# The output projection and first norm of a latent attention, moved into the block of its pairs

## The reference

```python
x = x + _layernorm(_L0_attn_ref(_layernorm(x), Wq_a, q_a_ln_w, Wq_b, Wkv_a, kv_a_ln_w, Wkv_b, Wo))
x = x + _layernorm(_L0_ffn_ref(_layernorm(x), ...))
...
# _L0_attn_ref: 32 heads, no mask but causal (1024 x 1024)
q = _rmsnorm(h @ Wq_a, q_a_ln_w) @ Wq_b                  # split in q_nope (128) and q_pe (64, rotary)
compressed, k_pe = split(h @ Wkv_a)                      # 64 + 64
kv = _rmsnorm(compressed, kv_a_ln_w) @ Wkv_b             # split in k_nope and v
probs = softmax(where(causal, q . k * scale, min))
return (probs @ v).reshape(s, 32 * 128) @ Wo
```

## Time and profile before

| | us |
|---|---|
| median of 3 runs (lowest, highest) | 1609.5 (1608.85, 1614.17) |
| profiled execution: span from its first to its last instruction | 1606.4 |
| difference of that median and that span | 3.1 |
| TensorE busy in the span | 1492.6 (93%) |
| VectorE, ScalarE, GpSimd busy | 1023.0, 821.6, 291.7 |

### The profile page before, as it was taken

The page is one execution under the profiler, slowest core; times in us unless marked ns, Lnnn a source line. Parts: engine busy times, 40 slices in busy tenths (PEclk is TensorE's granted clock), DMA queues, the critical chain, the costliest instruction groups (busy, mean ns, idle before and its releaser), DMA issues. The chain is left out here.

```text
span 1606.4 us, 22430 instructions
## 1 busy us (share of the span) xinstructions
PE 1492.6 (93%) x8030; PEld 981.8 (61%) x8030; DVE 1023.0 (64%) x2013; ACT 821.6 (51%) x1487; POOL 291.7 (18%) x276
## 2 busy tenths in 40 slices
PE   6866999999999999977979999899899999999998
PEld 4645777766677776656868888787453333333355
DVE  5744666666666666643553343364687998999646
ACT  5325666666666666632221212223316777777854
POOL 2762111111211111100000000001410243342221
PEclk9987999999999999998989999999998999999999
DMA  4142222121212221124312111105730444430001
GB/s 138 53 193 73 76 75 69 64 69 64 69 63 80 90 70 40 34 86 156 105 63 75 59 60 40 53 1 152 189 67 5 68 81 79 80 67 15 19 11 53
DMA packets 63154, 116.57 MB, mean 73 GB/s; under 512 B 12814, under 2 KB 32398, under 8 KB 61758
## 3 DMA queue, kind: packets, MB, share of 16 engines
q1 hardware_dynamic: 62692, 114.23, 24.4%
q10 hardware_dynamic: 288, 0.79, 0.3%
q0 software_dynamic: 64, 0.11, 0.0%
HBM read 82.78 MB, written 29.66 MB: 70 GB/s over the span
## 5 line engine op out<-in xcount | busy, mean ns | idle before, releaser
L1882 DVE TENSOR_REDUCE ah_minus_half<-ah_ring 128x1 f32<-128x512 f32 x512 | 321.8, 680 | 58.5 <-PE ah_ring L1788 57.1
L968 DVE CUSTOM_DVE_ANT_0 mh_score<-mh_score,mh_mask 128x128 f32<-128x128 f32 (+7 forms) x256 | 195.9, 765 | 179.1 <-PE mh_score L781 179.0
L1852 ACT ACTIVATE ah_probs<-ah_score 128x1024 f32<-128x1024 f32 x256 | 248.7, 1024 | 69.5 <-PE ah_score L1805 68.8
L890 ACT ACTIVATE mh_probs<-mh_score,mh_minus_max 128x128 f32<-128x128 f32 (+7 forms) x256 | 189.8, 741 | 39.7 <-DVE mh_minus_max L968 35.7
L1788 PE MATMUL ah_ring<-ah_k_stack,ah_q_stack 48*128 48x512 f32 x512 | 179.1, 464 | 13.9 <-DMA ah_k_stack<-qk_scratch 5.5
L1788 PEld LDWEIGHTS ah_ring<-ah_k_stack,ah_q_stack 48*128 48x128 f32 x512 | 79.0, 187 | 173.1 <-DVE ah_minus_half L1882 158.9
L1041 POOL TENSOR_TENSOR h_lo<-mh_pe,h_hi 64x512 fp32r<-64x512 f32 x64 | 81.8, 1278 | 459.0 <-ACT h_hi L876 455.4
L1805 PE MATMUL ah_score<-ah_q_stack,ah_k_stack 49*128 49x512 f32 x512 | 156.5, 444 | 4.6 <-DMA ah_q_stack<-ah_rows 2.9
L779 PE MATMUL mh_score<-shared,h_hi 128*128 128x512 f32 (+3 forms) x384 | 152.0, 396 | 3.0 <-ACT mh_probs L890 2.9
L1820 PE MATMUL ah_mix<-ah_probs,ah_v 128*32 128x512 f32 x1024 | 139.0, 615 | 0.6 <-ACT ah_probs L1852 0.6
L781 PE MATMUL mh_score<-shared,h_lo 128*128 128x512 f32 (+3 forms) x384 | 133.0, 346 | 0.0
(11 more groups left out here) (227 smaller groups left out, 2898.7 us busy)
## 6 DMA issues: line engine op xcount, KB each, us to landing
mh_w<-in_w_pairs SPq DMA_DIRECT2D x16, 896.0 KB, 5.6
x<-in_w_inner SPq DMA_DIRECT2D x14, 768.0 KB, 4.2
pe_scratch<-fr_pe_out SPq DMA_DIRECT2D x4, 2048.0 KB, 6.6
mh_pe<-pe_scratch SPq DMA_DIRECT2D x16, 512.0 KB, 4.0
mh_spread<-inverse_scratch SPq DMA_DIRECT2D x64, 128.0 KB, 2.9
a_scratch<-mh_mixed SPq DMA_DIRECT2D x32, 256.0 KB, 2.4
x<-a_scratch SPq DMA_DIRECT2D x8, 1024.0 KB, 6.3
qk_scratch<-ai_ring SPq DMA_DIRECT2D x32, 256.0 KB, 2.8
```

What stands on the lines that cost most here:

```text
L890: nc.scalar.activation(probs[:, s % 2, 0:width], score_ps[s % 2][:, base:base + width], ACT.Exp, bias=minus_max[:, s % 4:s % 4 + 1], scale ...
L968: nc.vector.tensor_tensor_reduce(out=scores, in0=scores, in1=mask[:, S - width:S], scale=-1.0, scalar=3e38, op0=ALU.add, op1=ALU.min, accu ...
L1852: nc.scalar.activation(probs[:, 2 * (u % 2) + c, :], score_ps[c][:].rearrange("p e n -> p (e n)"), ACT.Exp, scale=MHA_SCALE).then_inc(prob ...
L1882: nc.vector.reduce_max(minus_half[:, m:m + 1], ring[:, m % 3, :], AX.X, negate=True).then_inc(max_taken, 1)
```

## The change

`mla_output` no longer opens a block. It returns a function `finish`, which `mla_heads` calls before its own block is opened; what `finish` returns is issued at the end of each engine's list, in the same block. Semaphores of the heads are not cleared in between, and there is no meeting of the engines. The tiles of the output stage lie at fixed places over buffers of the heads that are dead by then: `a_hi` and `a_lo` of tile 0 over `w`, `absorbed_hi`, `absorbed_lo`, `pe32` and the probabilities of even slots; those of tile 1, and `x`, over `high_turned`. The two score tensors' first banks take the products, the two turn tensors the transposes. Each first use waits for the last reader of the old content (`high_free`, `low_probs_free`, `mixed_free`, `all_stored`). VectorE makes tile 0's `a_lo` before it takes the last pair's second half. `x` is loaded in two parts, tile 0 and the rest.

In the last pair alone three places move: the transposed inverse of the first half from slot 10 to 9, `mix_low` from slot 14 to 10, and VectorE's `take_mix` of that half from slot 15 to 13.

```diff
-            return (i + 1, 2) if half else (i, 11 if i == 0 else 10)
+            return (i + 1, 2) if half else (i, 11 if i == 0 else 9 if i == LAST else 10)
+        def low_at(i):
+            return 10 if i == LAST else 14
+        def take_low_at(i):
+            return 13 if i == LAST else SLOTS - 1
...
+        def low_probs_free(engine):
+            engine.wait_ge(turns_ready, groups_before(LAST, SLOTS - 1))
+        def high_free(engine):
+            engine.wait_ge(mix_ready, 2 * PAIRS)
+        def mixed_free(engine):
+            engine.wait_ge(mix_taken, 2 * PAIRS)
+        def all_stored(engine):
+            engine.wait_ge(mixed_out, 16 * 2 * PAIRS)
+        banks = ([ps[:, 0:BANK] for ps in score_ps], turn_ps)
+        finish_sync, finish_gpsimd, finish_tensor, finish_scalar, finish_vector, prepare_vector = finish(
+            ctx, first, banks, low_probs_free, high_free, mixed_free, all_stored)
+        block = ctx.enter_context(nc.Block())
...
             store(LAST, 1)
-            sp.wait_ge(mixed_out, 16 * 2 * PAIRS)
+            finish_sync(sp)
...
-                    if s == 14:
+                    if s == low_at(i):
                         mix_low(i)
...
             mix_high(LAST, 0, NT)
+            finish_tensor(pe)
...
-                    if s == SLOTS - 1:
+                    if s == take_low_at(i):
                         take_mix(i, 0)
             take_turned(LAST, SLOTS - 1)
             invert(LAST, 1)
+            prepare_vector(dve)
             take_mix(LAST, 1)
+            finish_vector(dve)
...
-    sem.clear()
...
+        x = at("x", [P, NT, D], 0)
+        a_hi = [at("a_hi0", [P, PAIRS, P], 32 * KB, F32R), at("a_hi1", [P, PAIRS, P], 16 * KB, F32R)]
+        a_lo = [at("a_lo0", [P, PAIRS, P], 40 * KB, F32R), at("a_lo1", [P, PAIRS, P], 24 * KB, F32R)]
...
+        def sync(sp):
+            def load_a(t):
+                if t == NT // 2:
+                    all_stored(sp)
+                sp.wait_ge(a_lo_ready, t - 1)
+                sp.dma_start(a_in[:, t % 2, :], a_scratch[t].rearrange("p i q -> p (i q)")).then_inc(a_loaded[t % 2], 16)
+            rows = io["x"].rearrange("(t p) d -> p t d", p=P)
+            high_free(sp)
+            sp.dma_start(x[:, 0:1, :], rows[:, 0:1, :]).then_inc(x_in[0], 16)
+            load_a(2)
+            sp.dma_start(x[:, 1:NT, :], rows[:, 1:NT, :]).then_inc(x_in[1], 16)
+            load_a(3)
...
+            def upper(t):
+                act.wait_ge(a_loaded[t % 2], 16 * (t // 2 + 1))
+                wait(act, y_ready, t - 1)
+                if t == 1:
+                    high_free(act)
+                nc.scalar.copy(flat(a_hi, t), a_in[:, t % 2, :]).then_inc(a_hi_ready, 1)
...
+        def prepare_vector(dve):
+            lower(dve, 0)
...
-                mla_heads(nc, io, ident, m, h, scratch["pe"], scratch["inverse"], scratch["a"])
-                mla_output(nc, io, ident, m, h, sides, w_in, flat_x, scratch["a"], x_dram_out)
+                finish = mla_output(nc, io, ident, m, h, sides, w_in, flat_x, scratch["a"], x_dram_out)
+                mla_heads(nc, io, ident, m, h, scratch["pe"], scratch["inverse"], scratch["a"], finish)
```

More of the change, by code:

```diff
@@ L935, in _ @@
             take_rows(LAST, 1)
+            finish_scalar(act)
         @block.vector
@@ L1072, in sync_work @@
[L1072 to L1093, removed]
+        KB = 1024
+        x = at("x", [P, NT, D], 0)
+        a_hi = [at("a_hi0", [P, PAIRS, P], 32 * KB, F32R), at("a_hi1", [P, PAIRS, P], 16 * KB, F32R)]
@@ L1114, in pool_work, with tensor, project, transposes @@
             nc.gpsimd.tensor_tensor(sides_lo[:].bitcast(F32R), sides_f[:], sides_hi[:], ALU.subtract).then_inc(sides_split, 1)
-        norm_block(nc, "n1", x, h, ident, out_dram=x_dram_out, project=project, x_dram=io["x"], scalar_work=scalar_work,
-                   vector_work=vector_work, sync_work=sync_work, projected=used, sync_first=sync_first, sync_each=sync_each,
-                   pool_work=pool_work)
+        def tensor(pe):
+            def project(t):
+                pe.wait_ge(a_lo_ready, t + 1)
+                wait(pe, y_used, t - 1)
+                products = [(a, w, i) for i in range(PAIRS) for a, w in ((a_hi, w_hi), (a_hi, w_lo), (a_lo, w_hi))]
+                for n, (a, w, i) in enumerate(products):
+                    last = nc.tensor.matmul(py[t % 2], a[t % 2][:, i, :], w[:, i, :], start=n == 0, stop=n == len(products) - 1)
+                last.then_inc(y_ready, 1)
+            def transposes(t):
+                pe.wait_ge(h_ready, t + 1)
+                wait(pe, ht_used, t - 1)
+                for k in range(ND):
+                    last = nc.tensor.transpose(pt[t % 2][:, k, :], hn[:, t % 2, k * P:(k + 1) * P], ident[:])
+                last.then_inc(ht_ready, 1)
+            for t in range(NT):
+                project(t)
+                if t:
+                    transposes(t - 1)
+            transposes(NT - 1)
@@ new lines, in scalar, with root @@
+        def scalar(act):
+            def upper(t):
[4 more added lines that the diff above has]
+                nc.scalar.copy(flat(a_hi, t), a_in[:, t % 2, :]).then_inc(a_hi_ready, 1)
+            def root(n):
+                act.wait_ge(var_ready, n + 1)
+                nc.scalar.activation(std[:, n % 2:n % 2 + 1], mv[:, n % 2, 1:2], ACT.Sqrt, bias=eps[:, 0:1]).then_inc(std_ready, 1)
+            upper(0)
+            upper(1)
+            for t in range(NT):
+                root(2 * t)
+                root(2 * t + 1)
+                if t + 2 < NT:
+                    upper(t + 2)
+                act.wait_ge(ht_ready, t + 1)
+                nc.scalar.copy(hT_hi[:, :, tile_of(t)], pt[t % 2][:]).then_inc(hi_ready, 1)
@@ new lines, in finish, with then, lower @@
+        done = [0]
+        def then(dve, instruction):
+            done[0] += 1
+            instruction.then_inc(dve_done, 1)
+            dve.wait_ge(dve_done, done[0])
+        def lower(dve, t):
+            if t == 0:
+                low_probs_free(dve)
+            dve.wait_ge(a_hi_ready, t + 1)
+            nc.vector.tensor_tensor(flat(a_lo, t), a_in[:, t % 2, :], flat(a_hi, t).bitcast(F32), ALU.subtract).then_inc(a_lo_ready, 1)
+        def prepare_vector(dve):
+            lower(dve, 0)
@@ L1121, in ffn_inner @@
+        return sync, gpsimd, tensor, scalar, vector, prepare_vector
+    return finish
 def ffn_inner(nc, io, h, sides, w_in, work, d, down_hi, down_lo):
```

84 lines of the change are left out of this document (67 added, 17 removed).

## The result

The changed kernel took 1591.04 us (median of 4 runs, 1587.73 to 1594.16), beside 1611.84 for the kernel before on the same chip: a ratio of 0.9868, 95% interval [0.9832, 0.9903]. So it is faster. The 13.1 us forecast would be a ratio of 0.9919: outside the first interval, inside the second, so the times alone do not settle whether the gain is larger than that.

A forecast was written before the change was run, and what follows sets the result against it. TensorE, busy 93% of the span, was taken as the bound, resting 15.8 us at the border of two blocks. Earlier projection 12.0 plus clock 1.1 made 13.1 us: 1596.4 against 1609.5 us, range 1592.5 to 1601.

The forecast's parts named there:

- What bounds the kernel, and the chain left by the change: Block border: tile 0 waits for multiplication, store, load, a_hi, a_lo; first projection at 719.1 instead of 731.04, 12.0 us sooner.
- The delay of 2.35 us let through at slot 10: Last pair's slots: mix_low moved to slot 10 delays what follows by 2.35 us, bounds 1.0 and 2.4.
- the one from the multiplication ahead of slot 15's maximum: VectorE, last pair: the early multiplication pushes that maximum to 705.77, 2.7 us later; mix_high ends at 716.9, hidden by the load.
- Tile 0's landing: Load after the border: issued at 708.1, tile 0 lands 6.7 us later, at 714.8.
- step 3: Store and load: first half's store issued at 705.8, 2.3 us sooner; load at 708.1; tile 0 landed at 714.8.
- The clock: First projection: 2.6 us lost at low clock before, 1.5 us still lost after, so 1.1 us back.
- a rest of 2.2 us: TensorE between last mixing and first projection: rests 2.2 us instead of 15.8, then a low-clock stretch costing 1.5 us.
- The rival with the clock up: First projection: clock stays up after the 2.2 us rest, 2.6 us back, 1594.9 us; chance 0.22.
- The tile loop: Loop over tiles: same matmuls in the same order, costed at nothing.
- The rival of slower matmuls: Tile loop: engines collide over banks, 384 matmuls slow from 0.223 to 0.27 us, 1614.4 us; chance 0.03.
- Next tiles late: First projection: loads and store meet, project(1) or project(2) waits, priced at 4 us, 1600.4 us; chance 0.06.
- The 3.1 us between span and time: Whole kernel: the median stands 3.1 us over the profiled span of 1606.4 us, added to the forecast span of 1593.3.

The follow-up runs named there:

- e8: e1 with 64 long-fulfilled waits put at the head of TensorE's list, so its code fetches come at other times; 1588.95 us (one run).
- e5: The changed kernel with the multiplication of the last pair's first half in slot 14 instead of 13; 1596.33 us, ratio 0.9915.
- e1: The changed kernel with the last pair's three places as before, so the merged block alone; 1599.55 us, ratio 0.9937.
- e4: The changed kernel with both pairs of a_hi and a_lo moved up by 32 bytes, off the multiple of 64; 1596.02 us, ratio 0.9906.
- e6: The changed kernel with the multiplication of the last pair's first half in slot 12 instead of 13; 1589.9 us, ratio 0.9887.
- e7: The changed kernel itself, measured a second time; 1593.29 us, ratio 0.9903.
- e9: The changed kernel with 150 long-fulfilled waits put at the head of TensorE's list; 1594.28 us (one run).
- e12: The changed kernel with 112 long-fulfilled waits put at the head of TensorE's list; 1599.59 us (one run).
- e3: The kernel before with a_hi and a_lo allocated ahead of the side factors, so they start on a multiple of 64 bytes; 1607.63 us, ratio 0.999.
- e10: The changed kernel with 164 long-fulfilled waits put at the head of TensorE's list; 1587.78 us (one run).
- e2: The kernel before, its border kept, with the last pair's three places moved as in the change; 1608.66 us, ratio 0.999.

## Why the prediction was right or wrong

- *What bounds the kernel, and the chain left by the change*: right. The store at 705.95 (forecast 705.8), loads at 708.26 (708.1), `a_hi` to projection 4.35 (4.27), the mixing's end at 716.94 (716.9), nothing behind it late. The delay of 2.35 us let through at slot 10 and the one from the multiplication ahead of slot 15's maximum are borne out by these two ends.
- *Tile 0's landing* (step 3, "tile 0 has landed 6.7 us later"): a mis-sized term, 1.6 us. I took the one row there was the earlier trace rows as the price of the load. It held a collision that this placement doesn't meet; e8 shows that without it 5.1 us is the price in e1's code. That the change doesn't meet it is luck: no part of the diff was made to move the instruction packets.
- *The clock* ("a rest of 2.2 us", 1.5 us for a low stretch): the rest did not come, and no run had one of 2.2 us there, so what such a rest costs stays open. With 3.19 us in e5, 4.67 in e8 and 6.54 in e1 the first projection ran low (7, 6 and 12 matmuls); with 1.49 and less, in the change, e4, e6, e7 and e9 to e12, it did not. As the load landed 1.6 us sooner, TensorE rested 0.83 us, and 2.4 us came back instead of 1.1. The rival with the clock up is what happened, for a reason it didn't name: a shorter rest, not a rest of 2.2 us at full clock. Its 1594.9 had the landing and the next term wrong as well.
- *The tile loop* ("has the same matmuls in the same order", costed at nothing): the step that failed outright, 2.1 us. The diff moved an operand from 32 bytes past a multiple of 64 to a multiple, and the mean distance fell by 0.0057 us, and there are 384 such matmuls. The rival of slower matmuls looked at the right place, with the wrong sign and the wrong cause (banks); e3 and e4 exclude the banks.
- *Next tiles late*: did not happen; the first projection's window is full (13.24 of 13.30 us) under DMA engines 0.70 busy, and so is the loop behind it.

The sum: 13.1 forecast, plus 1.6 (landing), 1.3 (clock) and 2.1 (address) makes 18.1, against 17.9 in the stretch. The range's low end, 1592.5, allowed for a clock that stays up and for one small gain besides, not for three terms that err the same way. The 3.1 us between span and time drop out of the difference; every run that has both on record shows 1.7 to 1.9 us, so the profiled execution before was probably some 1.3 us below its median.

The Trainium skill (TensorE: Matmul & The Clock Gate, HAM oscillation) has each wait between bursts pay anew, in a kernel whose waits are some 3 to 5 us long. The 3.19, 4.67 and 6.54 us of e5, e8 and e1 agree. The 0.83 us of the change are shorter than those waits, and did not pay.

## What to carry to other kernels

When a stage moves to other memory, compare where each loaded operand starts, before and after: two kernels with the same matmuls differed by 2.4% in their pace for 32 bytes. A transfer's duration from one row is one draw: look at what other queue was moving then before it is taken as the price. And what an earlier producer is worth depends on the wait behind it: here 2.4 us with the border in place and 6.6 without it (3.65 when the late landing is left out), so neither half alone tells what both bring.

## What was not expected of the hardware

- A 128x512 matmul whose loaded operand starts 32 bytes past a multiple of 64 follows the one before it after 0.2332 us, on a multiple after 0.2275 us (before and e4 against the change and e3).
- With a 16 KB packet of the instruction queue across the start of a 1 MB load, the load's last sixteenth landed at 6.7 to 7.3 us instead of 4.9 to 5.2 (before, e1, e3). With such a packet beside a 256 KB store, the store landed in 2.78 to 3.69 us instead of 2.27 to 2.64 (all runs; moved onto it in e9 and e10).
- The same rests went both ways. In the last slots of e2, TensorE rested 1.38 us, did eight transposes, rested 0.44 us, and from there was slow (0.89 and 1.06 us for four transposes each, 6.36 us for the mixing; granted clock 0.57 from 706.6 to 708.5). In the change it rested 1.39 and 0.44 us at the same places, and the same work took 0.63, 0.60 and 5.81 us, at 1.00. So the length of a rest alone does not tell whether the clock falls; why it fell in e2 stays open. Timeline of e2:

```profile
705.16 0.63 PE L790 MATMUL mh_turn<-ident,mh_probs 128*128 128x128 f32 x4 [1.38 <-DVE mh_high_turned L977]
705.62 0.60 PE L795 MATMUL mh_turn<-ident,mh_probs 128*128 128x128 f32 x4
706.66 0.89 PE L790 MATMUL mh_turn<-ident,mh_probs 128*128 128x128 f32 x4 [0.44 <-DVE mh_high_turned L977]
707.35 1.06 PE L795 MATMUL mh_turn<-ident,mh_probs 128*128 128x128 f32 x4
```

The two rows of the change that answer to the last two:

```profile
709.32 0.63 PE L815 MATMUL mh_turn<-ident,mh_probs 128*128 128x128 f32 x4 [0.44 <-DVE mh_high_turned L1004]
709.78 0.60 PE L820 MATMUL mh_turn<-ident,mh_probs 128*128 128x128 f32 x4
```
